# Second layer: all seven bins weighed by VectorE, all low halves taken by GpSimd, and all bins added as float32r pairs

## What is computed

```python
H = (x @ W).reshape(n, 4, 32).transpose(1, 0, 2)      # 4 heads of 32
s = H_s[:, src] + H_t[:, tgt]                          # a score per edge and head
s = jnp.where(s >= 0, s, 0.2 * s)
s = jnp.exp(s - jnp.max(s))
denom = zeros((4, n)).at[:, src].add(s)
alpha = s / (denom[:, src] + EPS)
agg = zeros((4, n, 32)).at[:, src].add(alpha[..., None] * H[:, tgt])
x = layernorm(x + elu(agg + x @ residual_projection))
```

## Time and profile before

| | |
|---|---|
| runs | 3259.9, 3257.95, 3258.22 us; median 3258.22 |
| profiled execution | span 3274.5 us (no other time of it is listed) |
| PE busy in the span | 3060.7 us, 93% |
| DVE busy | 3045.9 us, 93% |
| ACT busy | 2750.1 us, 84% |
| POOL busy | 155.0 us, 5% |

### The profile page before, as it was taken

How to read it: one execution, slowest core, us unless ns; L and a number is a source line. 1 busy time by engine, 2 the same in 40 slices (tenths; PEclk the granted TensorE clock), 3 DMA queues, 4 the chain that set the end, 5 groups by cost and what they waited for, 6 DMA issues and landing times. The chain is left out here.

```text
span 3274.5 us, 101508 instructions
## 1 busy us (share of the span) xinstructions
PE 3060.7 (93%) x40072; PEld 2792.8 (85%) x40072; DVE 3045.9 (93%) x4921; ACT 2750.1 (84%) x6946; POOL 155.0 (5%) x249
## 2 busy tenths in 40 slices
PE   5777699999999999699999999989999999999996
PEld 4666677778777877699999999988999999999994
DVE  8999889999999997799999999989999999999997
ACT  6988888888888885799999999987888888888887
POOL 0000000000000000000000000000111111111110
PEclk9989899999999997799999999999999999999998
DMA  3000022222222222234333333334455545554541
GB/s 66 13 14 11 23 98 93 87 93 94 93 87 93 94 86 48 65 96 97 97 97 96 97 96 97 97 93 137 161 163 160 164 161 163 161 163 161 162 151 41
DMA packets 173823, 333.06 MB, mean 102 GB/s; under 512 B 54876, under 2 KB 109616, under 8 KB 173264
## 3 DMA queue, kind: packets, MB, share of 16 engines
q1 hardware_dynamic: 170996, 323.30, 32.5%
q10 hardware_dynamic: 2348, 3.20, 0.4%
HBM read 320.77 MB, written 5.66 MB: 100 GB/s over the span
## 5 line engine op out<-in xcount | busy, mean ns | idle before, releaser
L1009 PE MATMUL l_gathered<-xp,l_src_onehot 128*128 128x128 bf16 x7203 | 467.0, 221 | 11.2 <-DVE l_src_onehot L922 11.2
L1436 PE MATMUL l_gathered<-hp,l_onehot 128*128 128x128 bf16 x7203 | 458.5, 219 | 0.0
L704 PE MATMUL sc_z<-sc_onehot,pq 128*128 128x256 f32 (+1 forms) x2450 | 429.4, 298 | 23.3 <-DVE sc_leaky L617 18.3
L1009 PEld LDWEIGHTS l_gathered<-xp,l_src_onehot 128*128 128x128 bf16 x7203 | 407.9, 99 | 26.3 <-DVE l_src_onehot L922 11.7
L788 ACT ACTIVATE sc_leaky<-sc_z 128x1024 f32<-128x1024 f32 (+3 forms) x325 | 309.8, 953 | 143.3 <-PE sc_z L708 140.5
L617 DVE SCALAR_TENSOR_TENSOR sc_leaky<-sc_z,sc_leaky 128x1024 f32<-128x1024 f32 (+3 forms) x325 | 370.1, 1139 | 60.0 <-ACT sc_leaky L788 52.5
L847 DVE TENSOR_TENSOR l_lane<-iota_b,l_lane_pairs 128x896 bf16<-128x896 bf16 x686 | 421.0, 614 | 0.0
L1436 PEld LDWEIGHTS l_gathered<-hp,l_onehot 128*128 128x128 bf16 x7203 | 406.1, 98 | 0.4
L708 PE MATMUL sc_z<-sc_onehot,pq 128*128 128x256 f32 (+1 forms) x2450 | 400.9, 286 | 0.0
L1450 PE MATMUL l_acc<-e,l_lane_wide 128*128 128x132 f32 x2744 | 385.5, 283 | 0.3 <-ACT e L1514 0.3
L704 PEld LDWEIGHTS sc_z<-sc_onehot,pq 128*128 128x128 f32 x2450 | 344.6, 196 | 35.9 <-issue 34.5
(11 more groups left out here) (246 smaller groups left out, 6107.4 us busy)
## 6 DMA issues: line engine op xcount, KB each, us to landing
rows_got<-edge_rows_wide SPq DMA_DIRECT2D x338, 448.0 KB, 3.7
l_got<-edge_rows_src SPq DMA_DIRECT2D x343, 224.0 KB, 3.2
placed<-edge_rows SPq DMA_DIRECT2D x144, 512.0 KB, 3.7
out_dram<-X SPq DMA_DIRECT2D x12, 256.0 KB
S<-edge_rows_wide SPq DMA_DIRECT2D x5, 448.0 KB, 8.4
edge_rows<-e SPq DMA_DIRECT2D x98, 6.1 KB
edge_rows_wide<-e SPq DMA_DIRECT2D x98, 12.2 KB
sc_last_rows<-edge_rows SPq DMA_DIRECT2D x24, 64.0 KB, 3.5
```

Source lines behind the costliest of these rows:

```text
L704: nc.tensor.matmul(z[:, b, 0:nw, :], PQ[:, b0 + b, q, 0:C], hot[:, r % HOTS, b, 0, 0:nw, :], start=(b == u and q == 0), stop=False)
L1009: ins = nc.tensor.matmul(gps[:, t % 2, i * P:(i + 1) * P], hot[:, t % RING, i, :], parts[:, g * GX + i, q, :], start=(q == 0), stop=(q == 2))
L1436: ins = nc.tensor.matmul(gps[:, t % 2, i * P:(i + 1) * P], dst_hot[:, t % RING, i, :], hp[:, g * GX + i, q, 0:C], start=(q == 0), stop=(q ...
```

## The change

- VectorE weighs all seven bins (128x896); ScalarE's `weigh_last` is gone.
- ScalarE rounds all seven bins; GpSimd takes the low halves of all seven (`take_low` moves from VectorE to GpSimd); all seven go to TensorE as float32r pairs, and the plain float32 matmuls are gone.
- The gather runs two steps ahead where it ran one; the scores run ten steps ahead on TensorE where they ran nine (VectorE made its one-hots ten ahead already, `t + AHEAD + 1`).
- `find_lanes` is of the same step instead of the next; the message buffer is free once the low halves are taken, where it was free once the messages were added.
- On GpSimd the all-reduce of block b + 1 stands before the low halves of step 5 of block b, the adds of block b - 1 behind those of step 4, and X is lowered in pieces of seven blocks, two of them at the start and the others behind the low halves of step 2 of blocks 1 to 5.
- The exponent of the next block stands ahead of the rounding on ScalarE, and the sums are taken two steps later.

```diff
-    NB, PER, AHEAD = NBK, NBK // GX, 9
+    NB, PER, AHEAD = NBK, NBK // GX, 10
-    RING = AHEAD + 2
+    RING = AHEAD + 1
-        halves, lows = sb("message_halves", [P, 2, SPLIT, 2, CW], F32R), sb("low_sums", [P, 2, CW])
+        halves, lows = sb("message_halves", [P, 2, GX, 2, CW], F32R), sb("low_sums", [P, 2, CW])
...
                     if t >= 2:
-                        dve.wait_ge(s["added"], t - 1)
-                    w = GX - 1
+                        dve.wait_ge(s["low"], t - 1)
                     nc.vector.tensor_tensor(
-                        msg[:, t % 2, 0:w, 0:C].rearrange("p i (e d) -> p i e d", e=HEADS),
+                        msg[:, t % 2, :, 0:C].rearrange("p i (e d) -> p i e d", e=HEADS),
...
-                def take_low(t):
-                    dve.wait_ge(s["high"], t + 1)
-                    nc.vector.tensor_tensor(halves[:, t % 2, :, 1, :], msg[:, t % 2, 0:SPLIT, :], halves[:, t % 2, :, 0, :],
-                                            ALU.subtract).then_inc(s["low"], 1)
...
-                    if 0 <= t + 1 < R:
-                        find_lanes(t + 1)
+                    if t >= 0:
+                        find_lanes(t)
...
-                pool.wait_ge(s["const"], 2)
-                for b in range(NB):
+                def find_all(b):
                     pool.wait_ge(s["top"], b + 1)
                     nc.gpsimd.partition_all_reduce(k.m_all[:, b:b + 1], top[:, b % 2:b % 2 + 1], P, RMAX).then_inc(s["all"], 1)
-                    if b >= 1:
+
+                def take_low(t):
+                    pool.wait_ge(s["high"], t + 1)
+                    nc.gpsimd.tensor_tensor(halves[:, t % 2, :, 1, :], msg[:, t % 2], halves[:, t % 2, :, 0, :], ALU.subtract
+                                            ).then_inc(s["low"], 1)
+
+                def lower(g):
+                    rows = X[:, g * GX:(g + 1) * GX, :].rearrange("p b c -> p (b c)")
+                    nc.gpsimd.tensor_scalar(rows, rows, -1.0, None, ALU.add)
+
+                lower(0)
+                lower(1)
+                pool.wait_ge(s["const"], 2)
+                find_all(0)
+                for t in range(R):
+                    b, g = divmod(t, PER)
+                    if g == PER - 2 and b + 1 < NB:
+                        find_all(b + 1)
+                    take_low(t)
+                    if g == 4 and b >= 1:
                         add_low(b - 1)
-                    nc.gpsimd.tensor_scalar(X[:, b, :], X[:, b, :], -1.0, None, ALU.add)
+                    if g == 2 and 2 <= b + 1 < PER:
+                        lower(b + 1)
...
                 def add_up(t):
                     b, g = divmod(t, PER)
-                    pe.wait_ge(s["messages"], t + 1)
-                    pe.wait_ge(s["weights"], t + 1)
                     pe.wait_ge(s["lane_wide"], t + 1)
...
                     pe.wait_ge(s["low"], t + 1)
-                    for i in range(SPLIT):
-                        last = g == PER - 1 and i == SPLIT - 1
+                    for i in range(GX):
                         ins = nc.tensor.matmul(acc[:, b % 2, 0:2 * CW], lane_wide[:, t % 2, i, :],
...
-                    if 0 <= t + 1 < R:
-                        gather(t + 1)
+                    if 0 <= t + 2 < R:
+                        gather(t + 2)
...
                 def take_high(t):
                     act.wait_ge(s["messages"], t + 1)
                     act.wait_ge(s["weights"], t + 1)
-                    nc.scalar.copy(halves[:, t % 2, :, 0, :], msg[:, t % 2, 0:SPLIT, :]).then_inc(s["high"], 1)
+                    if t >= 2:
+                        act.wait_ge(s["added"], t - 1)
+                    nc.scalar.copy(halves[:, t % 2, :, 0, :], msg[:, t % 2]).then_inc(s["high"], 1)
```

## The result

The changed kernel takes 4048.98 us (median of 4 runs, 4043.29 to 4050.37); the kernel before, beside it, takes 3258.15 (4 runs). The ratio is 1.2413 (95% interval 1.2381 to 1.2444): slower by 791 us, where 848 were forecast. The profiled execution took 4043.29 us, its span is 4041.4.

The account below looks back on a forecast made before the run. TensorE and VectorE were taken to share the bound; blocks of 37.4 us against 20.05 over 48 gaps gave 833 us, plus 15 once, so 3258 + 848 = 4106, said as 4105 (range 3840 to 4260).

Parts of the forecast that it names:

- The gap: On GpSimd, each block's stretch from the fifth step's low halves to the sixth's, around the all-reduce: 15.3 us.
- Change over: GpSimd idle while its code changes from ordinary arithmetic to the all-reduce: 6.5 us, between 5.99 and 7.40.
- change back: GpSimd idle while its code changes from the all-reduce to ordinary arithmetic: 7.6 us, between 6.0 and 8.64.
- The run of seven low halves: Rest of a block: two low halves back to back 4.1 us, five steps 17.0, TensorE's lower clock 1.0.
- The costs that come once: First change back before the first low halves, and X lowered in seven pieces: +15 us (5 to 30).
- The shared path: GpSimd's low halves and VectorE's lanes and one-hot exclude each other: 3.1 to 3.65 us a step.
- Rival 1: Code change stalls, but GpSimd and VectorE interleave inside long instructions or loads are near 6 us: 3866 to about 4000; chance 0.2.
- the loads don't stop the low halves: Rival: GpSimd's code stays in once both kinds ran, only the shared path costs: 3343 to 3563 us; chance 0.08.
- faster: Rival: neither stall nor exclusion holds, low halves take under 2.6 us every step, TensorE bounds: 3165 us; chance 0.05.
- The worse case (4): Rival: TensorE stays at 1.2 GHz through much of a block, or gaps are 17.6 us everywhere: about 4350; chance 0.09.
- The clock: TensorE restarts at its lower clock after each gap, adding up and gathering at half pace: 1.0 us a block (0 to 2).
- five steps at 3.4 us: The other five steps of a block follow at 3.1 to 3.65 us, taken as 3.4: 17.0 us.

Follow-up runs that it names:

- e2: Changed kernel with a second all-reduce in each block, over a column of ones, its result unused: 4520.17 us, ratio 1.3855.
- e1: Changed kernel with the all-reduce replaced by an ordinary GpSimd instruction that writes a zero shift: 3569.18 us, ratio 1.094.
- e4: e1 with VectorE's comparison of lanes left out from the third step on: 3320.52 us, ratio 1.0178.
- e7: e1 with GpSimd's low halves made to wait for VectorE's next one-hot: 3520.43 us, ratio 1.0801.
- e8: e6 with GpSimd's low halves made to wait for VectorE's next one-hot: 3282.8 us, ratio 1.0054.
- e6: Changed kernel without the all-reduce, GpSimd taking low halves of four bins, VectorE none, three bins plain float32: 3264.98 us, ratio 1.0012.
- e12: Changed kernel with all low halves moved to VectorE, behind its next one-hot, all-reduces kept: 3440.88 us, ratio 1.0549.

## Why the prediction was right

4105 was forecast (3840 to 4260) and 4049 measured, by the mechanism forecast. Point by point, a block being 36.1 us against 37.4:

- **The gap.** Forecast 15.3 us from the last low halves to the next; over the 48 blocks of GpSimd's timeline it is 14.9 in the mean (13.4 to 16.6). Change over 6.55 (5.71 to 7.74) for 6.5; change back 7.07 for 7.6, and 7.88 at the start, where the earlier trace rows had 8.64. One row read as support for it was thin: the all-reduce of the earlier trace rows starts only 0.57 us behind its maximum, so most of its 6.78 us would have passed in any case; e2, where nothing is waited for, is what shows the price. The rule of the Trainium skill (GPSIMD Engine Reference, Architecture, Instruction dispatch) of about 6 us for code loading fits the 5.88 of e2, is 0.6 us short of the way over here, and 1.1 us short of the way back; e2 adds that the stall comes at each change. By the 5.95 of the Trainium skill alone a gap would be 1.7 us shorter, 83 us over 48.
- **The run of seven low halves.** Forecast 4.1 + 17.0 + 1.0 = 22.1, measured 4.2 + 17.2 = 21.4 in the mean. One takes 2.15 us alone (forecast 2.0), two back to back 4.24. These two terms, 48 x (0.4 + 0.7) = 53 us, are nearly the whole of the 56 by which the forecast was high. The costs that come once, +15 in the sum, have 791 - 48 x 16.25 = 11 us left to them.
- **The shared path.** "That all of a 2 us instruction is held" was left open; it is: 0.61 becomes 1.57, 0.68 becomes 2.67, 0.26 becomes 2.23. The Trainium skill's sentence (SBUF — State Buffer, Who interferes with whom), that the one that starts first keeps the pair for the whole instruction, agrees with these rows. Rival 1, interleaving inside an instruction or loads near 6 us, falls with them and with the 6.55 and 7.07; so do "the loads don't stop the low halves" (2) and "faster" (3) with the 49 waits. The worse case (4) needed gaps of 17.6 us everywhere, and the longest was 16.6, or a low clock through much of a block, and in the block shown below it was back at 1.00 eight us after the restart.
- **The clock.** Forecast 1.0 us a block (0 to 2). TensorE waits 12.9 us for low halves in the gap. The windows behind it show 0.50 (1.2 GHz) for the 4 us from 3023, 0.75 for the next four and 1.00 for the seven from 3031, and the seven matmuls of adding up take 1.88 us at 3023 where they took 1.08 at 3003. Weigh waits for the gather in 96 places, 81.9 / 48 = 1.7 us a block. How much of this is the clock alone no run tells apart, nor how much of the 17.2 us above is.

```profile
3023.00:3027.00 4.00, 3.99 (x39) 3.90 (x40) 3.10 (x3) 2.08 (x4) 2.94 (x2) 0.50 0.02 4
3027.00:3031.00 4.00, 4.00 (x51) 3.89 (x50) 2.56 (x4) 1.72 (x3) 1.87 (x2) 0.75 0.39 115
```

- **The small prices.** Weigh 1.08 for 1.1; rounding 924 elements 0.96 for 0.98. (The range was given 0.78, though the two cases in it add up to 0.77.)
- **What was thought too low.** Not in the sum, but in its use: five steps at 3.4 us hold only between the gaps, which let two low halves start together, and only in the mean: single low halves start 2.1 to 5.05 us apart, where steps of 3 to 3.7 were to be seen. Without gaps the same program settles at 3.77 with the blocks' own work (e1), just above the 3.75 that the prediction had as the upper end for that. The 3.4 was a middle between two bounds, right for the case and wrong as a property of the step, so that here the number was partly luck; it cost the expectation of e1 its band.

The code change by itself is worth 480 us (e1). Of the other 310 the lanes' removal gives back 249 (e4), a wait that orders the two engines 49 (e7): both by one kernel against another, and neither is to be added to the other; 182 of the 249 are the lanes' own time on VectorE.

## What to carry to other kernels

Ask of an idle engine what its idle time is made of before giving it work in the loop: 6 to 8 us "issue" around a special instruction cost nothing while only late work hangs on that engine; once the chain ran through it they made 15 us a block, 10 of which reached the end. GpSimd work on SBUF that ran beside VectorE was paid, whole, by VectorE's next instruction that didn't read PSUM (here lanes, one-hot and the lift of the scores); put it where VectorE does something that reads PSUM, with a wait if need be, and make it no longer than that. A blocked instruction reads as a busy one, so a full VectorE may be a waiting one: compare the duration of one instruction with what it takes alone.

## What the runs showed of the hardware that was not expected

- The way over to the all-reduce took 6.55 us in the mean in the kernel after and 5.88 in e2 (L1408), the way back 7.07 and 7.05. Why the way over differs between the two, no run tells.
- A wait more on GpSimd made the kernel 49 us faster (e7 against e1), and the same wait gained nothing at four bins (e8 against e6).
- Two tiny float32 matmuls a block, of one row or one column, took TensorE about 0.31 us each, as much as two float32r bins of adding up.
- The all-reduce was 0.38 us long between GpSimd's own work (L1387, 375 to 378 ns), and 0.71 in the mean in e12, where VectorE is busy for 795.79 of 800 us. What stretches it there no run tells.
